# Turn 1 in an order of its own, one sum a slot later, and the transposition ahead of the last sum

## Chip, cores and metric

The kernel runs on one core of one Trainium2 chip. The metric is the device time of one execution in microseconds (us); lower is better.

## The reference

Input x has 8 sequences of 512 tokens with 128 features. Two layers follow one another, each of the form x = x + A(xn) + F(xn), with xn the layer norm of x.

```
layer 0, A: Mamba block.  proj = xn @ in_proj.T (256 + 256 columns); conv over 4 tokens, silu -> u
            x_dbl = u @ x_proj.T -> dt (64), B (16), C (16), each RMS-normed
            dt = softplus(dt @ dt_proj.T + b);  for each of 16 states n:
                h[t] = exp(dt*A_n)[t] * h[t-1] + (dt*u)[t] * B_n[t];   y += h * C_n
            y = (y + u*D) * silu(gate);  out = y @ out_proj.T
layer 0, F: 8 experts (128 -> 512 relu -> 128), each token goes to the one with the largest gate logit
layer 1, A: attention, 16 heads of 8, window of 32 tokens to each side
layer 1, F: silu(x @ wg.T) * (x @ wu.T) @ wd.T, hidden size 384
```

## The kernel before

Every engine has one program, written by one generator of units: `units(it)` yields (name, k, b), unit name with index k for sequence b, and each engine's program emits for each unit what it has to do (or nothing). So one list gives the order of work on TensorE, VectorE, ScalarE, POOL and the DMA queue of SP alike. Engines wait for one another by semaphores.

A lead computes the first layer norm and the expert routing. Then come turns. In turn `it` several sequences are worked on, each at another stage (`LAG`): the lane "pre" prepares sequence it+1 (convolution, u, dt, dtu, B and C rows), "scan" runs the 16 states of sequence it, "attn" runs layer 1 of sequence it-1, and "finish" ends sequence it-2. A turn has 28 slots. `plan()` makes the list of units of each slot from tables, and `PLAN_AT` is that list. `STEP_AT` gives the slot of each of the 16 scan steps, `SUM_AT` the slot of each sum; `EDGE` is the order of slot 0; `HEAD`, `MID` and `REST` place the small units; `SUM_LAST` names the slots in which the sum stands behind row maximum and turn instead of ahead of them.

One state n of the scan goes through these units:

- "step": ScalarE computes the decays dA of state n+1 (line 1105, two instructions), VectorE scans state n (line 884, hst <- dA, dBu).
- "product": VectorE computes dBu of state n+1 (line 876), and POOL computes hc = hst * C (line 1286). It waits until that dBu is done and, since hc has two buffers, until sum n-2 is done.
- "sum": TensorE adds hc into the two banks of y by 8 transposes (line 1389). The last one, of state 15, is "y_end" in slot 0 of the next turn; "gated" (VectorE, line 976) multiplies y by the gate, "yT" (line 1462) transposes it, "init" (line 1380) starts the next y and "out" (line 1471) is the output projection.
- "spread": SP loads the B and C rows of state n+3 into the ring bcr; it waits for product n-1.

Units of "pre": xnT transposes the sequence's input (TensorE, line 1398; ScalarE copies it), hs0 and hs1 are the convolved input projection (TensorE, lines 1406 and 1409), th0 and th1 their tanh (ScalarE, line 1117), u0 and u1 (VectorE, line 904), zg0 and zg1 the gate projection (TensorE, line 1415; its tanh "tg" on ScalarE, line 1122), xdr (VectorE, line 925), dtT, dtp and so on. All of these use one PSUM bank in turn. `take0` lets xnT wait also for the last "fh" (VectorE, line 1041) of the turn before:

```
            if key == "xnT":
                done1(eng, b + LAG["pre"] - 1 - LAG["attn"], f"up{HC - 1}")
```

Units of "attn": x1 adds x_res and the output projection (VectorE, line 980), ln_a the statistics (VectorE, and rstd on POOL, line 1315), ln_b the normalised rows (ScalarE, line 1156; TensorE, line 1478), q and k (TensorE, line 1482; ScalarE), kin the transfer of k into its blocks (SP, line 698), v0 to v3 (TensorE, line 1489). Then 16 blocks, one a slot from slot 5 on: "scores" (TensorE, lines 1502 and 1504, with the values of an earlier block, line 1443), "rowmax" (VectorE, line 1025, nmax), "exp" (ScalarE, line 1185, pexp), "turn" (TensorE, line 1522; ScalarE copies, line 1198). fg, fs, fu and fh are the feed-forward part (lines 1537, 1203, 1036, 1041).

x_res is the input of the sequence plus the experts' rows: "slots" computes the row numbers (VectorE) and loads the input (SP, line 708), "rows" are four indirect transfers of POOL that add the experts' rows to it (line 1267).

Turn 0 has no layer 1 yet; the 40 expert tiles run beside its scan. It also has four slots more, in which scan steps 0 to 4 of sequence 1 are done ahead (`AHEAD`), with sums 0 to 2. So turn 1 skips these and its scan restarts at step 5 in slot 5. For sequence 0, "clear" (VectorE clears kT, line 855, and prepares bias rows), "slots" and "rows" are issued at the end of slot 0 of turn 1, once all expert tiles are stored. The last turn has a list of its own and no scan.

## Time and profile before

| | |
|---|---|
| median of 3 timed runs | 990.7 us (987.13 to 991.66) |
| profiled execution | 994.0 us, of it 992.2 us span from the first to the last instruction |
| TensorE clock granted, mean | 0.926 of full |
| busy: TensorE, VectorE, ScalarE, POOL | 83%, 76%, 64%, 47% |
| turns 2 to 6 | about 95 us each, starting near 350, 446, 544, 638, 733 us |
| turn 1 | from 246 to about 350 us |

The time is that of whole executions; the profile is one further execution, and all positions are counted from its span's start. Busy says how long an engine worked, not that it set the time: which engine waits for which in a stretch says that.

### The profile page before, as it was taken

How to read it: one execution, taken by the hardware profiler on the slowest of the kernel's cores; microseconds unless marked ns; L12 is line 12 of the kernel's file. 1: busy time of each engine (PE TensorE's matmuls, PEld its weight loads, DVE VectorE, ACT ScalarE, POOL GpSimd, SP SyncE). 2: the span in 40 equal slices, each digit the busy share in tenths (PEclk: the TensorE clock that was granted, in tenths of full speed). 3: DMA queues.
4: the chain of work that ended last, by engine and by line, in shares of the span. 5: the costliest groups of instructions: out<-in, count | busy, mean ns of one | idle time of the engine just before them, and what ended most of it. 6: DMA issues, size and time to landing. Idle time of an engine off the chain costs nothing.

```text
span 992.2 us, 15627 instructions
## 1 busy us (share of the span) xinstructions
PE 819.9 (83%) x5226; PEld 566.6 (57%) x5226; DVE 749.5 (76%) x1051; ACT 636.4 (64%) x1976; POOL 462.9 (47%) x256
## 2 busy tenths in 40 slices
PE   4746789767499888989897989898989897888876
PEld 4523787656365456556655665665566555556544
DVE  8719654627258889798879988888889888886577
ACT  1114567535278867875797779667947794885555
POOL 4275242213437447644764575348445843664100
PEclk9967999989699899998899999899989998899898
DMA  8436699785324244424532443444344525551100
GB/s 264 170 102 180 218 281 298 231 239 168 74 68 105 72 109 133 98 72 126 144 92 79 137 132 77 107 118 126 70 110 123 118 59 131 123 132 32 23 1 22
DMA packets 85951, 123.19 MB, mean 124 GB/s; under 512 B 8560, under 2 KB 43760, under 8 KB 85744
## 3 DMA queue, kind: packets, MB, share of 16 engines
q1 hardware_dynamic: 79584, 115.38, 42.2%
q0 software_dynamic: 6288, 6.82, 3.1%
q8 instruction: 42, 0.69, 0.3%
q14 instruction: 37, 0.30, 0.1%
HBM read 106.21 MB, written 12.29 MB: 119 GB/s over the span
## 4 chain that ended last, share of the span: by engine, by line
PE 38%; DVE 23%; issue 15%; POOL 11%; ACT 9%; DMA 3%; DVEq 0%; SPq 0%; POOLq 0%; ACTq 0%
DVE hst L884 8%; POOL hc L1286 6%; PE more L1522 5%; DVE dBu L876 4%; PE y_bank L1389 4%; ACT pexp L1185 3%; POOL xs_d L1252 2%; ACT dA L1105 2%; PE y_bank L1380 2%; PE work L1504 2%; PE work L1409 2%; PE work L1435 1%; POOL x_res L1267 1%; PE work_l L1504 1%; PE work L1415 1%
## 5 line engine op out<-in xcount | busy, mean ns | idle before, releaser
L1286 POOL TENSOR_TENSOR hc<-hst,bcr 128x1024 f32<-128x1024 f32 x124 | 303.3, 2446 | 371.1 <-DVE dBu L876 354.8
L884 DVE TENSOR_TENSOR_SCAN hst<-dA,dBu 128x1024 f32<-128x1024 f32 x128 | 291.7, 2279 | 1.1 <-issue 0.3
L876 DVE TENSOR_TENSOR dBu<-dtu,bcr 128x1024 f32<-128x1024 f32 x128 | 164.8, 1288 | 19.3 <-DMA bcr<-bc_d 9.9
L1105 ACT ACTIVATE dA<-dt,neg_a 128x511 f32<-128x511 f32 x256 | 170.7, 725 | 7.9 <-issue 4.4
L1389 PE MATMUL y_bank<-pk,hc 128*128 128x128 f32 x1024 | 142.9, 284 | 31.4 <-POOL hc L1286 31.4
L1389 PEld LDWEIGHTS y_bank<-pk,hc 128*128 128x128 f32 x1024 | 118.6, 145 | 60.6 <-POOL hc L1286 39.4
L1522 PE MATMUL more<-pk,pexp 128*96 128x128 f32 x480 | 111.4, 297 | 26.1 <-ACT pexp L1185 16.9
L1522 PEld LDWEIGHTS more<-pk,pexp 128*96 128x96 f32 x480 | 56.9, 126 | 79.6 <-issue 35.6
L1198 ACT COPY pT<-more 96x512 f32<-96x512 f32 x120 | 69.8, 582 | 23.0 <-PE more L1522 22.8
L1185 ACT ACTIVATE pexp<-work,nmax 128x96 f32<-128x96 f32 x240 | 77.8, 335 | 10.2 <-DVE nmax L1025 10.2
L1185 ACT ACTIVATE pexp<-work_l,nmax 128x96 f32<-128x96 f32 x240 | 78.5, 346 | 4.3 <-DVE nmax L1025 4.3
L1025 DVE TENSOR_REDUCE nmax<-work 128x4 f32<-128x384 f32 x60 | 33.3, 555 | 50.8 <-PE work L1443 41.6
L1409 PE MATMUL work<-xnT,pk 128*128 128x512 f32 x128 | 63.0, 638 | 0.0
L1267 POOL DMA_INDIRECT x_res<-ys_d,slot_b x32 | 56.1, 1754 | 6.0 <-issue 5.3
L1185 ACT ACTIVATION_READ_ACCUMULATOR pexp<-work_l,nmax 128x1 f32 x240 | 50.8, 211 | 0.0
L1504 PE MATMUL work<-kT,qbd 128*128 128x384 f32 x120 | 49.9, 498 | 0.0
L1504 PE MATMUL work_l<-kT,qbd 128*128 128x384 f32 x120 | 49.2, 492 | 0.0
L1185 ACT ACTIVATION_READ_ACCUMULATOR pexp<-work,nmax 128x1 f32 x240 | 48.2, 201 | 0.0
L1409 PEld LDWEIGHTS work<-xnT,pk 128*128 128x128 f32 x128 | 26.9, 210 | 30.0 <-issue 29.2
L1117 ACT ACTIVATE z<-work 128x512 f32<-128x512 f32 x16 | 9.6, 599 | 48.6 <-PE work L1409 43.8
L1025 DVE TENSOR_REDUCE nmax<-work_l 128x4 f32<-128x384 f32 x60 | 32.9, 548 | 8.4 <-PE work_l L1443 8.2
L1122 ACT ACTIVATE tg<-work 128x512 f32<-128x512 f32 x16 | 9.7, 604 | 31.9 <-PE work L1415 31.9
(367 smaller groups left out, 1562.5 us busy)
## 6 DMA issues: line engine op xcount, KB each, us to landing
bcr<-bc_d SPq DMA_DIRECT2D x128, 512.0 KB
qbd<-in_wx SPq DMA_DIRECT2D x8, 578.0 KB
o_all<-in_wx SPq DMA_DIRECT2D x8, 578.0 KB
pT<-in_wx SPq DMA_DIRECT2D x8, 578.0 KB
kT<-in_wx SPq DMA_DIRECT2D x8, 578.0 KB, 4.9
vw<-in_wx SPq DMA_DIRECT2D x8, 578.0 KB, 5.3
xs_d<-dA POOLq DMA_DIRECT2D x1, 2560.0 KB, 12.2
hst<-in_hidden SPq DMA_DIRECT2D x8, 256.0 KB, 4.0
```

The source lines that it names most:

```text
L876: v.tensor_tensor(dBu[:], dtu[par], bcr[n % RING][:, 0:1, :].to_broadcast([P, NH, L]), ALU.mult).then_inc(s_dBu, 1)
L884: v.tensor_tensor_scan(hst[n % 2][:].rearrange("p h t -> p (h t)"), dA[n % 2][:].rearrange("p h t -> p (h t)"), dBu[:].rearrange("p h t -> ...
L1025: v.tensor_reduce(nmax[:, k, :], w1k(b, f"s{k}")[:, 0:RG * KW].rearrange("p (r k) -> p r k", r=RG), AX_X, ALU.max, negate=True).then_inc(s ...
L1105: s.activation(dA[n % 2][:, h, 1:L], dt[par][:, h, 1:L], ACT.Exp, scale=neg_a[:, h, n:n + 1]).then_inc(s_dA, 1)
L1185: last = s.activation(pexp[k % 2][:, r, :], w1k(b, f"s{k}")[:, r * KW:(r + 1) * KW], ACT.Exp, bias=nmax[:, k, r:r + 1], accum_out=den[:, r ...
L1198: s.copy(pT[k % 4][:], w1k(b, f"pT{k}")[0:KW, :]).then_inc(free1(b, f"pT{k}"), 1)
L1267: g_.indirect_dma_start(x_res[:, j, :], None, ys_d.rearrange("i j p d -> (i j p) d"), bass.IndirectOffsetOnAxis(ap=slot_b[:, j:j + 1], axi ...
L1286: g_.tensor_tensor(hc[n % 2][:], hst[n % 2][:], bcr[n % RING][:, 1:2, :].to_broadcast([P, NH, L]), ALU.mult).then_inc(s_hc, 1)
L1389: last = t.matmul(y_bank[h][:, q], hc[n % 2][:, h, q], ident, is_transpose=True, start=False, stop=(n == N - 1 and j == NT - 1))
L1409: last = t.matmul(bank0[:], w_k[:, k, q], xnT[:, k:k + L], start=False, stop=(k == KC - 1))
L1504: last = t.matmul(w1k(b, key)[:, 0:RG * KW], qbd[:, k, :, :].rearrange("p h q -> p (h q)"), kT[:, :, k * GQ:k * GQ + KW], start=False, sto ...
L1522: last = t.transpose(w1k(b, key)[0:KW, r * P:(r + 1) * P], pexp[k % 2][:, r, :], ident)
```

## The change

It has three parts.

1. Turn 1 gets a plan of its own (`plan_one`, `PLAN_ONE`). Scan steps 5 to 9 stand in slots 0 (5), 1 (6 and 7), 2 (8) and 3 (9), step 5 ahead of the experts' rows of sequence 0; steps 10 to 15 stand in slots 5, 6, 8, 10, 12 and 14. Sums 3 to 7 stand in slots 0 to 3, sums 8 to 13 in the slots of step m+2, sum 14 in slot 16. hs1, th1 and u1 move into slot 1, ahead of x1, q and k. The order of slot 0 is now: sum 3, the edge units, slots, step 5, product 5, spread 5, rows, clear. Clearing now stands behind the rows and behind scan 5.
2. In all turns, sum 7 moves from slot 10 to slot 11, again as the last of the scan and attention units of its slot.
3. In slot 0 of all turns, "xnT" moves ahead of "y_end" and "rdT".

```
--- before.py
+++ after.py
@@ -68,8 +68,8 @@
 SLOTS = 28
 ATTN_AT = 5
 STEP_AT = (0, 1, 2, 3, 4, 5, 6, 8, 10, 12, 14, 16, 18, 20, 22, 23)
-SUM_AT = {m: 1 if m == 0 else STEP_AT[m] + 2 for m in range(N - 1)}
-EDGE = [("attn", "y_end"), ("finish", "rdT"), ("pre", "xnT"), ("attn", "gated"), ("attn", "yT"), ("scan", "init"), ("attn", "out"), ("pre", "hs0")]
+SUM_AT = {m: 1 if m == 0 else STEP_AT[m] + (3 if m == 7 else 2) for m in range(N - 1)}
+EDGE = [("pre", "xnT"), ("attn", "y_end"), ("finish", "rdT"), ("attn", "gated"), ("attn", "yT"), ("scan", "init"), ("attn", "out"), ("pre", "hs0")]
 HEAD = {1: [("attn", "x1", 0), ("attn", "ln_a", 0)], 22: [("attn", "fg", 0), ("attn", "fu", 0)]}
 MID = {2: [("scan", "slots", 0)], 8: [("pre", "ss", 0)], 10: [("pre", "xdr", 0)], 18: [("pre", "dw", 0)], 20: [("pre", "dt", 0)], 23: [("pre", "dtu", 0)]}
 REST = {1: [("pre", "th0", 0), ("pre", "u0", 0), ("attn", "ln_b", 0)],
@@ -88,7 +88,7 @@
         24: [("attn", "fs", 2), ("attn", "fh", 2), ("attn", "rden", 0)], 25: [("pre", "start", 0)]}
 ROWMAX_FIRST = (5, 6)
 ROWMAX_MID = (8, 20)
-SUM_LAST = (7, 8, 10)
+SUM_LAST = (7, 8, 11)
 O_LAG = 3
 HEADS_AT = 1
 O_LAST = 4
@@ -101,7 +101,7 @@
 LAG = {"pre": -1, "scan": 0, "attn": 1, "late": 2, "finish": 2}
 
 
-def plan():
+def plan(step_at, sum_at):
 
     def of(kind, slot):
 
@@ -113,7 +113,7 @@
     slots = []
     for slot in range(SLOTS):
         units = []
-        n = STEP_AT.index(slot) if slot in STEP_AT else None
+        n = step_at.index(slot) if slot in step_at else None
         if slot == 0:
             units += [(lane, name, 0) for lane, name in EDGE]
         units += HEAD.get(slot, [])
@@ -130,7 +130,7 @@
         if n is not None:
             units.append(("scan", "product", n))
         units += [(lane, "averages", g) for lane, g in of("values", slot)]
-        sums = [("scan", "sum", m) for m in range(N - 1) if SUM_AT[m] == slot]
+        sums = [("scan", "sum", m) for m in range(N - 1) if sum_at[m] == slot]
         units += sums if slot not in SUM_LAST else []
         if slot not in ROWMAX_FIRST + ROWMAX_MID:
             units += [(lane, "rowmax", g) for lane, g in of("scores", slot)]
@@ -143,8 +143,32 @@
     return slots
 
 
-PLAN_AT = plan()
+PLAN_AT = plan(STEP_AT, SUM_AT)
 PLAN = [unit for units in PLAN_AT for unit in units]
+
+
+def plan_one():
+
+    steps = {10: 5, 11: 6, 12: 8, 13: 10, 14: 12, 15: 14}
+    step_at = [steps.get(n, SLOTS) for n in range(N)]
+    sum_at = {m: step_at[m + 2] if m + 2 in steps else 16 if m == N - 2 else SLOTS for m in range(N - 1)}
+    slots = plan(step_at, sum_at)
+
+    def scan(n):
+
+        return ("scan", "step", n), ("scan", "product", n), ("scan", "spread", n)
+    step, product, spread = zip(*[scan(n) for n in range(N)])
+    slots[0] = [("scan", "sum", 3)] + slots[0] + [("first", "slots", 0), step[5], product[5], spread[5]] + [
+        ("first", "rows", j) for j in range(NT)] + [("first", "clear", 0)]
+    slots[1] = [("pre", "th0", 0), ("scan", "sum", 4), step[6], ("pre", "u0", 0), ("pre", "hs1", 0), product[6], spread[6],
+                ("pre", "th1", 0), ("scan", "sum", 5), step[7], ("pre", "u1", 0), ("attn", "x1", 0), ("attn", "ln_a", 0),
+                product[7], spread[7], ("attn", "ln_b", 0)]
+    slots[2] = [("attn", "q", 0), ("attn", "k", 0), step[8], ("scan", "slots", 0), product[8], ("scan", "sum", 6), spread[8]]
+    slots[3] = [("attn", "kin", 0), ("attn", "v0", 0), ("attn", "v1", 0), step[9], product[9], ("scan", "sum", 7), spread[9]]
+    return slots
+
+
+PLAN_ONE = plan_one()
 
 
 def last_turn():
@@ -231,7 +255,6 @@
             put(0, slot, ("up", m))
         if 1 <= m <= NM:
             put(0, slot, ("down", m - 1))
-    put(1, 0, ("clear", 0), ("slots", 0), *[("rows", j) for j in range(NT)])
     return at
 
 
@@ -575,7 +598,10 @@
                 for name, k, b in LAST:
                     yield name, k, b, (B - b) % 2
             for slot in range(0 if it >= B else SLOTS_0 if it == 0 else SLOTS):
-                for lane, name, k in PLAN_AT[slot] if slot < SLOTS else []:
+                for lane, name, k in (PLAN_ONE if it == 1 else PLAN_AT)[slot] if slot < SLOTS else []:
+                    if lane == "first":
+                        yield name, k, 0, 0
+                        continue
                     if it == 1 and (name, k) in DONE_AHEAD:
                         continue
                     b = it - LAG[lane]
```

## Rows read from the trace of the kernel before

**Rows 1.** The page's busy table: busy us, share of the span, instructions.

```profile
PE 819.9 (83%) x5226; PEld 566.6 (57%) x5226; DVE 749.5 (76%) x1051; ACT 636.4 (64%) x1976; POOL 462.9 (47%) x256
```

**Rows 2.** Windows: PE, PEld, DVE, ACT, POOL busy us (instructions), clock, DMA.

```profile
249.00:284.00 35.00, 22.73 (x87) 14.54 (x86) 7.42 (x27) 11.81 (x20) 9.59 (x8) 0.71 0.29 69
...
284.00:303.00 19.00, 16.24 (x118) 11.13 (x117) 18.76 (x23) 14.69 (x56) 12.86 (x7) 1.00 0.26 66
303.00:328.00 25.00, 24.84 (x176) 14.09 (x176) 19.66 (x21) 23.09 (x92) 14.86 (x8) 1.00 0.49 109
328.00:346.00 18.00, 14.17 (x84) 7.86 (x83) 16.02 (x14) 15.22 (x43) 7.06 (x3) 0.81 0.21 67
```

**Rows 3.** VectorE's timeline, front of turn 1: start, us, line, operation, [idle before].

```profile
249.03 1.98 DVE L855 MEMSET kT<- 128x2304 f32 x1 [0.43 <-issue]
...
265.42 0.69 DVE L980 TENSOR_TENSOR x1r<-x_res,work 128x512 f32<-128x512 f32 x1 [12.27 <-DMA x_res<-ys_d,slot_b]
...
280.39 0.69 DVE L904 SCALAR_TENSOR_TENSOR u<-z,work 128x512 f32<-128x512 f32 x1 [12.02 <-ACT z L1117]
284.47 2.28 DVE L884 TENSOR_TENSOR_SCAN hst<-dA,dBu 128x1024 f32<-128x1024 f32 x1
286.85 1.23 DVE L876 TENSOR_TENSOR dBu<-dtu,bcr 128x1024 f32<-128x1024 f32 x1
```

**Rows 4.** Timelines of TensorE, SP and POOL, front of turns 1 and 2.

```profile
251.36 3.75 PE L1471 MATMUL work<-pk,dtu 128*128 128x128 f32 x16 [0.77 <-ACT dtu L1152]
...
276.05 3.60 PE L1409 MATMUL work<-xnT,pk 128*128 128x512 f32 x8
...
355.57 1.95 PE L1471 MATMUL work<-pk,dtu 128*128 128x128 f32 x16
...
277.61 2.54 SPq L698 DMA_DIRECT2D kT<-rbuf  x4
...
255.63 0.19 POOL L1266 TENSOR_TENSOR tick_p<-one 128x1 f32<-128x1 f32 x1 [4.78 <-DMA x_res<-in_hidden]
```

**Rows 5.** TensorE's timeline, sum 7 and block 7, turns 3 and 5.

```profile
491.98 1.97 PE L1389 MATMUL y_bank<-pk,hc 128*128 128x128 f32 x8 [2.09 <-POOL hc L1286]
...
498.29 0.33 PE L1502 MATMUL work_l<-bandb,identb 128*128 128x384 bf16 x1
...
683.40 1.09 PE L1389 MATMUL y_bank<-pk,hc 128*128 128x128 f32 x8 [2.25 <-POOL hc L1286]
...
687.52 0.34 PE L1502 MATMUL work_l<-bandb,identb 128*128 128x384 bf16 x1
```

**Rows 6.** VectorE's timeline at the same place in turn 3.

```profile
490.02 0.66 DVE L925 TENSOR_TENSOR xdr<-work,rr 128x256 f32<-128x256 f32 x3
490.60 2.42 DVE L876 TENSOR_TENSOR dBu<-dtu,bcr 128x1024 f32<-128x1024 f32 x1
...
497.91 0.56 DVE L1025 TENSOR_REDUCE nmax<-work 128x4 f32<-128x384 f32 x1 [4.43 <-PE work L1443]
```

**Rows 7.** Timelines at turn 3's edge, and one row of turn 2's.

```profile
445.48 1.10 PE L1389 MATMUL y_bank<-pk,hc 128*128 128x128 f32 x8 [2.33 <-POOL hc L1286]
...
446.97 1.06 PE L1398 MATMUL work<-pk,x_in 128*128 128x128 f32 x4
...
445.49 0.69 DVE L1041 TENSOR_TENSOR fh<-fsg,work 128x512 f32<-128x512 f32 x1
...
447.67 1.27 DVE L976 TENSOR_TENSOR dtu<-y_bank,sg 128x512 f32<-128x512 f32 x2
...
351.14 0.63 PE L1398 MATMUL work<-pk,x_in 128*128 128x128 f32 x4
```

**Rows 8.** Chain of waits, end of turn 1: start, us, what.

```profile
335.74 1.24 ACT dA L1105 x2
...
349.71 0.12 DVE fh L1041
...
351.90 0.69 DVE dtu L976
```

More of the change, by code:

```diff
@@ L70 @@
 STEP_AT = (0, 1, 2, 3, 4, 5, 6, 8, 10, 12, 14, 16, 18, 20, 22, 23)
-SUM_AT = {m: 1 if m == 0 else STEP_AT[m] + 2 for m in range(N - 1)}
-EDGE = [("attn", "y_end"), ("finish", "rdT"), ("pre", "xnT"), ("attn", "gated"), ("attn", "yT"), ("scan", "init"), ("attn", "out"), ("pre", "hs0")]
+SUM_AT = {m: 1 if m == 0 else STEP_AT[m] + (3 if m == 7 else 2) for m in range(N - 1)}
+EDGE = [("pre", "xnT"), ("attn", "y_end"), ("finish", "rdT"), ("attn", "gated"), ("attn", "yT"), ("scan", "init"), ("attn", "out"), ("pre", "hs0")]
 HEAD = {1: [("attn", "x1", 0), ("attn", "ln_a", 0)], 22: [("attn", "fg", 0), ("attn", "fu", 0)]}
@@ L90 @@
 ROWMAX_MID = (8, 20)
-SUM_LAST = (7, 8, 10)
+SUM_LAST = (7, 8, 11)
 O_LAG = 3
@@ L101, with plan @@
 LAG = {"pre": -1, "scan": 0, "attn": 1, "late": 2, "finish": 2}
-def plan():
+def plan(step_at, sum_at):
     def of(kind, slot):
@@ L115, in plan @@
         units = []
-        n = STEP_AT.index(slot) if slot in STEP_AT else None
+        n = step_at.index(slot) if slot in step_at else None
         if slot == 0:
@@ L132, in plan @@
         units += [(lane, "averages", g) for lane, g in of("values", slot)]
-        sums = [("scan", "sum", m) for m in range(N - 1) if SUM_AT[m] == slot]
+        sums = [("scan", "sum", m) for m in range(N - 1) if sum_at[m] == slot]
         units += sums if slot not in SUM_LAST else []
@@ L143, in plan, with plan_one, scan @@
     return slots
-PLAN_AT = plan()
+PLAN_AT = plan(STEP_AT, SUM_AT)
 PLAN = [unit for units in PLAN_AT for unit in units]
+def plan_one():
+    steps = {10: 5, 11: 6, 12: 8, 13: 10, 14: 12, 15: 14}
+    step_at = [steps.get(n, SLOTS) for n in range(N)]
+    sum_at = {m: step_at[m + 2] if m + 2 in steps else 16 if m == N - 2 else SLOTS for m in range(N - 1)}
+    slots = plan(step_at, sum_at)
+    def scan(n):
+        return ("scan", "step", n), ("scan", "product", n), ("scan", "spread", n)
+    step, product, spread = zip(*[scan(n) for n in range(N)])
+    slots[0] = [("scan", "sum", 3)] + slots[0] + [("first", "slots", 0), step[5], product[5], spread[5]] + [
+        ("first", "rows", j) for j in range(NT)] + [("first", "clear", 0)]
+    slots[1] = [("pre", "th0", 0), ("scan", "sum", 4), step[6], ("pre", "u0", 0), ("pre", "hs1", 0), product[6], spread[6],
+                ("pre", "th1", 0), ("scan", "sum", 5), step[7], ("pre", "u1", 0), ("attn", "x1", 0), ("attn", "ln_a", 0),
+                product[7], spread[7], ("attn", "ln_b", 0)]
+    slots[2] = [("attn", "q", 0), ("attn", "k", 0), step[8], ("scan", "slots", 0), product[8], ("scan", "sum", 6), spread[8]]
+    slots[3] = [("attn", "kin", 0), ("attn", "v0", 0), ("attn", "v1", 0), step[9], product[9], ("scan", "sum", 7), spread[9]]
+    return slots
+PLAN_ONE = plan_one()
 def last_turn():
@@ L233, in early @@
             put(0, slot, ("down", m - 1))
-    put(1, 0, ("clear", 0), ("slots", 0), *[("rows", j) for j in range(NT)])
     return at
@@ L577, in units @@
             for slot in range(0 if it >= B else SLOTS_0 if it == 0 else SLOTS):
-                for lane, name, k in PLAN_AT[slot] if slot < SLOTS else []:
+                for lane, name, k in (PLAN_ONE if it == 1 else PLAN_AT)[slot] if slot < SLOTS else []:
+                    if lane == "first":
+                        yield name, k, 0, 0
+                        continue
                     if it == 1 and (name, k) in DONE_AHEAD:
```

## The prediction

> **What bounds the kernel now.** I read the page's busy table first. TensorE is busy 83% and VectorE 76% of the span [rows 1], so neither fills it, and the question is where each waits. I then cut the span at the turns and cut turn 1 finer [rows 2]. It has three parts. From 249 to 284 us VectorE works 7.4 of 35 us and TensorE's mean clock is 0.71: nobody is the bound there, a chain of waits is. From 284 to 303 VectorE works 18.8 of 19. From 303 to 328 TensorE works 24.8 of 25. From 328 to 346 no engine is full, and the chain of waits passes through ScalarE and VectorE.
>
> The first part is a pause of the scan. VectorE waits 12.3 us until the experts' rows are in x_res, does x1 and the statistics, waits 12.0 us for the second tanh (its input projection stands behind q and k on TensorE [rows 4]), and runs scan 5 only at 284.47, behind the row maximum of block 0 [rows 3]. The later turns have no such hole, but have a smaller one of their own. In turn 3 sum 7 keeps TensorE idle 2.09 us, the work behind it runs at half speed (sum 1.97 us, against 1.09 in turn 5), and VectorE waits 4.43 us for block 6 [rows 5, 6]. I find this wait in turns 2 to 6, at half speed after it in all but turn 5. At the turn's edge TensorE waits again, 2.33 us, for the last product of POOL [rows 7].
>
> **Part 1, the own order of turn 1.** Nothing is taken away; five scans (2.28 us) with their five dBu (1.23 us), 17.5 us of VectorE, move from slots 5 to 23 into the 24.3 us in which VectorE idles [rows 3]. Five products of POOL and five pairs of decays (1.24 us each on ScalarE) [rows 8] move too, and SP's five ring loads. What may be late through this is x1. Ahead of it on VectorE now stand, from 248.7 on, scan 5, dBu 6, the clearing (the 1.98 us memset and some 2 us of small copies [rows 3]), scan 6, u0, dBu 7, scan 7 and u1. Their own times are 3 x 2.28 + 2 x 1.23 + 4 + 2 x 0.68 = 14.7 us, so 263.4 without waits. With the waits for the two tanh I get 265.0 to 266, against 265.42 now. On POOL product 5 (2.35 us) comes after dBu 6, at 252.5, and is done at 254.9; the rows start at 255.6 as before [rows 4]. Product 6 follows them at 263.6 to 266, ahead of rstd, which wants the statistics at 267.8. On SP load 8 is queued behind the load of x_res, load 9 waits for product 5. Loads 10 and 11 wait for products 6 and 7 and stand ahead of kin; product 7 is done at about 271.5, and kin waits until 277.6 for k anyway. So rows, x1 and layer norm keep their times within 1 us.
>
> The second projection (3.60 us [rows 4]) then no longer stands between k and v0, which would give 4 us. But the kin transfers are issued from 277.61 for 2.54 us [rows 4] and I take some 2 us more for the last to land, so block 0 can't start before 282.1 against 282.98. ScalarE has two more pairs of decays among the copies, and scan 9 with dBu 10 stands ahead of row maximum 0. I take a gain of 0.3 us for the front; the bounds are a loss of 3.5 (that scan and dBu fully exposed) and a gain of 0.9.
>
> From 284 to 303 the slots hold the same work as before with other step numbers, and VectorE is full: no gain. At slot 10 the sum is now one whose product is two steps old. TensorE's wait of 2.1 us there goes, but VectorE's slow dBu 9 (2.42 us) is next, and row maximum 5 gates exp 5. I work out 1.0 us for slots 10 and 12.
>
> Slots 16 to 23 lose all scans. The chain of waits passes there through two pairs of dA (1.24 us each [rows 8]), a table load, and two scans with a dBu each (2.28 and 1.23 us [rows 3]). I walked the stretch again without them, each engine in order. exp 13 starts 0.95 us earlier, exp 15 2.9, fg1 4.1. The last fh, now at 349.71, would end at 344.95 instead of 350.40. Behind it rden and dBu 0 take 1.7 us, and gated comes at 346.7 against 351.9 [rows 8]: 5.2 us. It is ScalarE, exp by exp and two table loads, that now sets this pace. Bounds: 2 us (if TensorE falls to half speed in the thinner stretch, where it is busy 14.2 of 18 us already [rows 2]) and 7 us. Part 1 is 0.3 + 1.0 + 5.2 = 6.5 us, from 0 to 9.
>
> **Part 2, sum 7 one slot later.** In turn 3 xdr ends near 490.7 [rows 6]. The gate projection can then start, block 6 follows to 492.9, and row maximum 5 ends at 493.5 (dBu 9 ends at 493.0 [rows 6]). exp 5 and turn 5 end at 495.1, sum 7 at 496.0, and block 7 starts there instead of 498.29 [rows 5]: 2.3 us. VectorE's second row maximum comes 4 us earlier, but from here TensorE is the bound as in turn 1, so 2.3 is the gain. Product 9 on POOL needs sum 7 and can't start before dBu 10, near 498, so nothing is late. In turn 5, at full speed, the same walk puts block 7 at 687.4 against 687.52 [rows 5]: 0.1 to 0.2 us. So almost all of this part is the clock, and it is worth something only where the two short waits that stay (0.9 us for xdr, 1.0 us for exp 5) don't bring it down too. Turn 1 and turn 5 show that 2.1 to 2.3 us idle sometimes leaves it up. I take three of four turns kept up: 3 x 2.3 + 2 x 0.2 = 7.3 us, bounds 1 and 9.6. Turns 0 and 7 have no such wait: nothing.
>
> **Part 3, transposition ahead of the last sum.** The time of 4 transposes (0.63 us at full, 1.06 at half speed) goes from behind the sum to before it. But xnT first waits for the last fh (take0), and that ends at 446.18 in turn 3, while the last sum now starts at 445.48 [rows 7]. The sum then starts at 446.8 and ends at 447.8 at best; gated on VectorE now starts at 447.67, freed by dBu. So full speed costs 0.2 us. In turns 3, 5 and 6 the transposes already run at half speed (1.06 us [rows 7]); there the idle stretch grows from 2.33 to 3.0 us, and if sum and transposes both are slow the sum ends near 449 and gated is 1.2 us late. In turn 2 there is nothing to wait for after part 1. I take 3 x 1.2 + 0.2 = 3.8 us of loss, bounds 0 and 6. The earlier copy on ScalarE gives nothing back: hs0, its reader, runs after init and out.
>
> The Trainium skill ("TensorE: Matmul & The Clock Gate", Part 1) says that TensorE is throttled to half by default and that activity releases it. By that rule part 3, which lengthens an idle stretch, costs its upper bound at each edge (rival (c)), and part 2 pays; the trace agrees in that four of five waits at sum 7 are followed by half speed.
>
> **Sum.** 6.5 + 7.3 - 3.8 = 10.0 us less. The profiled execution took 994.0 us around a span of 992.2, so it would be 984.0; the three timed runs have a median of 990.7, 3.3 lower, and I forecast 990.7 - 10.0 = 980.7.
>
> **Rivals.** (a) The clock falls at sum 7's place anyway, since the waits for xdr and exp 5 take its place: part 2 gives 1, and 990.7 - 6.5 - 1 + 3.8 gives 987. For it speaks that 1.9 of 2.1 us idle stay; against it that they are split. (b) Everything goes well: the clock stays up at sum 7 in all four turns and at the edges nothing is lost, 6.5 + 9.6 - 0.2 gives 974.8; with front and end of turn 1 at their best, 972. For it: the edges of turns 2 and 4 ran at full speed. (c) The other side: low clock at the turn's edge. If every one of five edges drops and stays low through the output projection (3.75 us at half speed in turn 1, 1.95 at full in turn 2 [rows 4]), an edge costs 1.3 + 1.8 = 3.1 us, 15.5 in all, against 13.8 gained: 992; with part 2 lost as well, 999. It decides from 2.8 us an edge. Against it: in turn 3 the projection is at full speed again. (d) The front of turn 1 eats its gain: decays 9 and scan 9 put row maximum 0 3.5 us later, and the end of the turn is held by half speed at 2: turn 1 gives nothing and the time is 990.7 - 7.3 + 3.8 = 987.
>
> **How the numbers follow.** Forecast 0.53, (a) 0.17, (b) 0.12, (c) 0.08, (d) 0.10. 0.5% is 5.0 us, about what a measurement of this kernel can tell from no change: faster is below 985.7, slower above 995.7. The forecast's own range is 974 to 986; nearly all of it and (b) are faster, some 0.1 of (a) and (d) too: 0.74. Slower is the worse half of (c) and a little more, 0.06; the rest, 0.20, is the same. The range for 8 in 10 runs from (b) to a little above (a) and (d): 972 to 989.
>
> **What would show it.** In the profile after: scans 5 to 9 of turn 1 before 284 and row maximum 0 at 283 to 285; no scan after slot 14, and the first gated of turn 2 near 346 instead of 351.9; no TensorE wait of 2.1 us on sum 7, and L1415's waits (ACT tg) down; turns 2 to 6 some 1 to 2 us shorter each than 95; before the last sum of each turn a wait of 3 us that now ends with the transposes, freed by fh. Wrong would be: x1 after 267; half speed in the gate projections in spite of the move; the span from the last fh to gated longer by more than 1.5 us.

## The result, and the profile after

The changed kernel took 981.98 us (median of 20 runs, 977.26 to 991.18), the kernel before 989.11 us (20 runs, 983.83 to 994.0). The ratio is 0.9935 with a 95% interval of 0.9912 to 0.9957: 6.4 us by the ratio (4.3 to 8.7), 7.1 by the medians, so it is faster by a small amount that is clear of the noise. The forecast was 980.7, inside a range of 972 to 989. The experiments below show that the total came near for reasons that are not those of the sum: one term was worth nothing, one about 12 us where 7.3 was forecast, and one cost 6 to 10 us where 3.8 was.

The profiled execution took 983.53 us. First the page of the changed kernel: the span, the busy table, and the group of the sums.

```profile
span 981.7 us, 15627 instructions
...
PE 808.1 (82%) x5226; PEld 557.4 (57%) x5226; DVE 757.3 (77%) x1051; ACT 638.4 (65%) x1976; POOL 466.8 (48%) x256
...
L1415 PE MATMUL y_bank<-pk,hc 128*128 128x128 f32 x1024 | 139.4, 279 | 9.8 <-POOL hc L1312 9.5
```

The same group of before has this row on its page (lines of the changed kernel are 26 higher from `plan_one` on).

```profile
L1389 PE MATMUL y_bank<-pk,hc 128*128 128x128 f32 x1024 | 142.9, 284 | 31.4 <-POOL hc L1286 31.4
```

TensorE's idle time ahead of the sums fell from 31.4 to 9.8 us. That is 21.6 us of waits gone for 6.4 us of time: a wait that goes is not time that is won. The count of instructions is as in [rows 1]; TensorE is busy 11.8 us less with the same work, so part of it ran faster, and the mean granted clock is 0.943 against 0.926.

**Front of turn 1.** VectorE's timeline (start, duration, line, operation, idle time before it), to be held against [rows 3].

```profile
248.01 2.35 DVE L1085 TENSOR_TENSOR slot_b<-slot_f,one 128x4 uint32<-128x4 f32 x1
...
254.36 1.98 DVE L881 MEMSET kT<- 128x2304 f32 x1 [0.47 <-issue]
...
268.04 0.69 DVE L930 SCALAR_TENSOR_TENSOR u<-z,work 128x512 f32<-128x512 f32 x1 [3.21 <-ACT z L1143]
268.65 0.68 DVE L1006 TENSOR_TENSOR x1r<-x_res,work 128x512 f32<-128x512 f32 x1
...
282.97 2.29 DVE L910 TENSOR_TENSOR_SCAN hst<-dA,dBu 128x1024 f32<-128x1024 f32 x1 [6.27 <-ACT dA L1131]
...
287.35 0.56 DVE L1051 TENSOR_REDUCE nmax<-work 128x4 f32<-128x384 f32 x1 [0.76 <-PE work L1530]
```

And two rows of TensorE: the bias rows of the second input projection with the wait ahead of them, and the projection, hs1.

```profile
261.43 0.61 PE L1432 MATMUL work<-onesb,conv_rows 96*128 96x512 bf16 x1 [4.82 <-DVE u L930]
261.83 5.47 PE L1435 MATMUL work<-xnT,pk 128*128 128x512 f32 x8
```

Scans 5 to 9 now do stand ahead of the attention blocks; VectorE's hole is filled. But x1 comes at 268.65 against 265.42, and row maximum 0 at 287.35 against 283.99. Counted from the last add of the experts (247.81 here, 248.32 before), x1 is 3.7 us later (20.84 against 17.1) and row maximum 0 is 3.9 us later (39.54 against 35.67). The chain to read is hs1, then the second tanh, then u1, then x1. The projection takes 5.47 us, part of it at half speed, where it took 3.60 [rows 4]; it stands behind 4.82 us in which TensorE waits for u0 (the one PSUM bank of this lane is free only then). u1 waits 3.21 us for its tanh, and x1, whose data could have come sooner, stands directly behind u1 on the same engine.

**Turn 1 after that.** Windows of the changed kernel, columns as in [rows 2].

```profile
248.00:287.00 39.00, 25.45 (x119) 16.36 (x118) 28.02 (x37) 18.73 (x32) 20.77 (x13) 0.82 0.45 111
...
287.00:306.00 19.00, 17.34 (x127) 11.35 (x125) 18.41 (x22) 14.66 (x56) 14.54 (x8) 1.00 0.45 108
...
306.00:331.00 25.00, 22.94 (x160) 12.37 (x152) 15.43 (x19) 20.86 (x87) 13.74 (x7) 1.00 0.35 74
...
331.00:347.00 16.00, 12.62 (x68) 5.33 (x67) 8.00 (x11) 12.54 (x40) 0.00 (x0) 0.89 0.00 1
```

Its last fh and the first gated of turn 2, on VectorE:

```profile
347.27 0.69 DVE L1067 TENSOR_TENSOR fh<-fsg,work 128x512 f32<-128x512 f32 x1
...
349.60 0.69 DVE L1002 TENSOR_TENSOR dtu<-y_bank,sg 128x512 f32<-128x512 f32 x1
```

The last window (16 us against 18 in [rows 2]) has no POOL work and half the VectorE work: all scans are out of it. From row maximum 7 (312.03, before 309.58) to the last fh (347.27, before 349.71 [rows 8]) it is 35.24 us against 40.13, 4.9 us less, where 5.2 was forecast. The middle gained 0.9, where 1.0 was forecast. In all, this one execution has turn 1 1.8 us shorter: 101.79 us from the last add to gated, against 103.58.

**Sum 7.** TensorE's timeline at that place in turn 3, against [rows 5].

```profile
486.81 1.16 PE L1441 MATMUL work<-pk,xnT 128*128 128x128 f32 x8 [0.85 <-DVE xdr L951]
487.80 0.33 PE L1528 MATMUL work<-bandb,identb 128*128 128x384 bf16 x1
...
490.17 1.19 PE L1548 MATMUL more<-pk,pexp 128*96 128x128 f32 x4 [1.04 <-ACT pexp L1211]
491.20 1.04 PE L1415 MATMUL y_bank<-pk,hc 128*128 128x128 f32 x8
492.07 0.33 PE L1528 MATMUL work_l<-bandb,identb 128*128 128x384 bf16 x1
```

The 2.09 us wait is split into 0.85 for xdr and 1.04 for exp 5, as walked, and sum 7 takes 1.04 us instead of 1.97. In turn 5 the clock fell in spite of the move: the gate projection there takes 2.08 us instead of the 1.16 of turn 3.

```profile
675.25 2.08 PE L1441 MATMUL work<-pk,xnT 128*128 128x128 f32 x8 [1.02 <-DVE xdr L951]
```

**The edge.** TensorE's timeline at turn 3's edge and turn 4's, against [rows 7].

```profile
440.62 1.08 PE L1424 MATMUL work<-pk,x_in 128*128 128x128 f32 x4 [3.13 <-issue]
441.50 1.91 PE L1415 MATMUL y_bank<-pk,hc 128*128 128x128 f32 x8
...
537.01 0.63 PE L1424 MATMUL work<-pk,x_in 128*128 128x128 f32 x4 [3.12 <-issue]
537.47 1.04 PE L1415 MATMUL y_bank<-pk,hc 128*128 128x128 f32 x8
```

The idle stretch is 3.13 us instead of 2.33. The profile names no releaser for it, but the transposes start 0.1 us behind the end of the last fh (440.52), for which they wait in the program. At turn 3's edge the transposes run at half speed behind it, and now the last sum does too: 1.91 us against 1.10. From the end of the last fh to gated it is then 2.9 us (440.52 to 443.45), against 1.5 before: late by 1.4. The low clock behind gated is not new at this edge, though. These are the windows of the 7 us from gated on in the changed kernel and in the kernel before:

```profile
443.45:450.45 7.00, 6.34 (x33) 6.20 (x33) 4.71 (x4) 3.88 (x7) 2.10 (x1) 0.54 0.38 101
```

```profile
447.67:454.67 7.00, 6.54 (x36) 6.20 (x35) 4.71 (x5) 4.21 (x7) 2.11 (x1) 0.58 0.60 152
```

At turn 4's edge both run at full speed behind an idle stretch of the same length.

The time from each gated to the next puts this together. "Half" is what the mean clock of that stretch says of time at half speed: 2 x (1 - clock) x length.

| turn | 2 | 3 | 4 | 5 | 6 | sum |
|---|---|---|---|---|---|---|
| before, us | 95.77 | 97.20 | 94.02 | 95.09 | 96.27 | 478.35 |
| before, half | 7.8 | 12.7 | 4.5 | 6.3 | 10.9 | 42.2 |
| after, us | 93.85 | 95.10 | 92.72 | 96.26 | 94.69 | 472.62 |
| after, half | 3.8 | 6.5 | 0.5 | 10.9 | 5.9 | 27.6 |

A turn that ran wholly at full speed takes some 92.5 us, and every turn above that has stretches at half speed. Turn 5, the one that kept its clock at sum 7 before, lost it there after, and became slower by 1.2 us. So a single profile cannot price these edits. That is why each part was timed by itself.

### The profile page after: what moved, and what is told of

Same layout as the page of the kernel before. It is cut to its first block, busy times and chain, and to the rows that moved or that the text cites. A ratio compares the mean times of both kernels' runs of the same rounds, so it can differ in the third digit from the quotient of the medians.

```text
span 981.7 us, 15627 instructions
## 1 busy us (share of the span) xinstructions
PE 808.1 (82%) x5226; PEld 557.4 (57%) x5226; DVE 757.3 (77%) x1051; ACT 638.4 (65%) x1976; POOL 466.8 (48%) x256
## 4 chain that ended last, share of the span: by engine, by line
PE 49%; DVE 20%; issue 10%; ACT 9%; DMA 4%; POOL 4%; SPq 3%; DVEq 0%; POOLq 0%; ACTq 0%
DVE hst L910 8%; PE y_bank L1415 6%; PE more L1548 6%; PE work L1435 4%; DVE dBu L902 3%; ACT pexp L1211 3%; POOL xs_d L1278 2%; PE y_bank L1406 2%; PE work L1530 2%; PE work_l L1530 2%; DMA bcr<-bc_d 2%; DVE nmax L1051 2%; PE work L1461 2%; ACT dA L1131 1%; PE work L1497 1%
## 5 line engine op out<-in xcount | busy, mean ns | idle before, releaser
L902 DVE TENSOR_TENSOR dBu<-dtu,bcr 128x1024 f32<-128x1024 f32 x128 | 168.2, 1314 | 18.5 <-DMA bcr<-bc_d 9.6
L1415 PE MATMUL y_bank<-pk,hc 128*128 128x128 f32 x1024 | 139.4, 279 | 9.8 <-POOL hc L1312 9.5
L1435 PE MATMUL work<-xnT,pk 128*128 128x512 f32 x128 | 65.7, 661 | 0.0
L1293 POOL DMA_INDIRECT x_res<-ys_d,slot_b x32 | 60.2, 1882 | 5.7 <-issue 5.6
L1441 PE MATMUL work<-pk,xnT 128*128 128x128 f32 x128 | 20.6, 311 | 11.8 <-DVE xdr L951 10.4
```

The costliest lines, as they stand in the source:

```text
L902: v.tensor_tensor(dBu[:], dtu[par], bcr[n % RING][:, 0:1, :].to_broadcast([P, NH, L]), ALU.mult).then_inc(s_dBu, 1)
L1293: g_.indirect_dma_start(x_res[:, j, :], None, ys_d.rearrange("i j p d -> (i j p) d"), bass.IndirectOffsetOnAxis(ap=slot_b[:, j:j + 1], axi ...
L1415: last = t.matmul(y_bank[h][:, q], hc[n % 2][:, h, q], ident, is_transpose=True, start=False, stop=(n == N - 1 and j == NT - 1))
L1435: last = t.matmul(bank0[:], w_k[:, k, q], xnT[:, k:k + L], start=False, stop=(k == KC - 1))
```

## The experiments

All kernels compute the whole reference. "Zeros" in some of them are matmuls that add zero to y. The time is the median of the runs, the ratio is to the kernel before with its 95% interval, the clock is the median over the runs of the mean granted clock.

### Each part alone

The first three kernels tell which terms of the sum hold. Part 2 alone (e1):

```
+SUM_AT = {m: 1 if m == 0 else STEP_AT[m] + (3 if m == 7 else 2) for m in range(N - 1)}
+SUM_LAST = (7, 8, 11)
```

> The kernel before with part 2 alone: sum 7 in slot 11 instead of 10, in all turns. Theory (the wait at sum 7 costs through TensorE's clock): the wait of 2.1 us before sum 7 is gone in turns 2 to 6, the gate projection of these turns runs at full speed in at least three of four turns that had half speed, and the time falls by 5 to 9 us (ratio 0.991 to 0.995). Rival (the wait is only handed on to xdr and exp 5, and the gain of the changed kernel is from turn 1 and the later clock): the time falls by 0 to 2 us, and the gate projections stay at half speed. In both, turn 1 keeps its pause.

Part 3 alone (e2):

```
+EDGE = [("pre", "xnT"), ("attn", "y_end"), ("finish", "rdT"), ("attn", "gated"), ...
```

> The kernel before with part 3 alone: xnT ahead of the last sum and rdT. Theory (xnT waits for the last fh, and so holds up the last sum): TensorE idles about 3 us instead of 2.3 at the edges of turns 3 to 6, gated is released by the sum instead of standing behind dBu, 0.2 us later at full and 1.3 us later at half speed; the time grows by 1 to 4 us (ratio 1.001 to 1.004). Rival (the place of the four transposes makes no difference, since gated stands behind dBu anyway): within 1 us. A third way, that the earlier copy on ScalarE helps, would make it shorter by 1 to 2 us.

Part 1 alone (e3) is `plan_one` with SUM_AT, SUM_LAST and EDGE as before.

> The kernel before with part 1 alone: the own order of turn 1. From the trace of the changed kernel, x1 comes 3.2 us late and row maximum 0 3.4 us late, slots 10 and 12 give 0.9 and the end of the turn 4.9, so the first gated of turn 2 comes 2.3 us sooner: 2 to 3 us less in all (ratio 0.997 to 0.998). Rival (the front's loss belongs to the edge's new order or to a chance state of the clock in that one profile): row maximum 0 near 284 and 5 to 7 us less in all.

| | us (runs) | ratio | clock |
|---|---|---|---|
| before | 988.21 (22) | | 0.9335 |
| e1, part 2 alone | 977.58 (6) | 0.9877 [0.984, 0.9913] | 0.943 |
| e2, part 3 alone | 998.95 (6) | 1.0104 [1.0064, 1.0144] | 0.9195 |
| e3, part 1 alone | 989.05 (12) | 1.0014 [0.9984, 1.0044] | 0.935 |

Part 2 gives 12 us (8.6 to 15.8 by its interval) where 7.3 was forecast; the upper bound of 9.6 lies inside the interval. Part 3 costs 10 us (6.3 to 14.2) where 3.8 was forecast, above its bound of 6. Part 1 gives nothing that can be told from zero where 6.5 was forecast. The expectations of the first two were missed on the high side too (5 to 9 and 1 to 4 us), and e3's 2 to 3 us did not come. Without part 3 the change would be a better one; that is tried below.

Where part 2's surplus lies can be read by cutting each turn in three at rows of VectorE: from gated to row maximum 5, from there to row maximum 8 (sum 7 and what stands behind it), and from there to the next gated. In turn 3 of the kernel before, whose gated is at 447.67, and then of part 2 alone:

```profile
492.93 0.54 DVE L1025 TENSOR_REDUCE nmax<-work_l 128x4 f32<-128x384 f32 x1
...
503.21 0.56 DVE L1025 TENSOR_REDUCE nmax<-work 128x4 f32<-128x384 f32 x1
```

```profile
444.76 1.28 DVE L976 TENSOR_TENSOR dtu<-y_bank,sg 128x512 f32<-128x512 f32 x2
...
487.79 0.54 DVE L1025 TENSOR_REDUCE nmax<-work_l 128x4 f32<-128x384 f32 x1
...
495.76 0.56 DVE L1025 TENSOR_REDUCE nmax<-work 128x4 f32<-128x384 f32 x1 [1.44 <-PE work L1443]
```

The same readings, in us, for turns 2 to 6 one by one; the last two columns are summed over them:

| | gated to row maximum 5 | to row maximum 8 | to the next gated | sum |
|---|---|---|---|---|
| before | 44.71, 45.26, 43.02, 45.47, 45.46 | 9.64, 10.28, 9.58, 8.09, 9.38 | 207.46 | 478.35 |
| e1, part 2 alone | 44.72, 43.03, 43.03, 43.34, 44.71 | 7.97, 7.97, 7.97, 7.97, 7.98 | 207.07 | 465.76 |
| e2, part 3 alone | 44.72, 46.40, 45.07, 45.30, 43.03 | 9.58, 9.64, 8.10, 10.29, 9.48 | 209.91 | 481.52 |
| after | 43.03, 45.57, 43.04, 44.98, 45.31 | 7.97, 7.97, 7.97, 9.14, 7.97 | 209.67 | 472.62 |

At sum 7 the kernel before loses 2.3 us in turn 3, which is what the prediction worked out for this place, 1.4 to 1.7 in turns 2, 4 and 6 and 0.1 in turn 5: part 2 gains 7.1 us there. The windows of the 8 us that hold sum 7 in turn 3 show the clock, before and then with part 2 alone:

```profile
490.00:498.00 8.00, 6.02 (x29) 4.50 (x30) 3.57 (x7) 3.42 (x13) 7.72 (x4) 0.57 0.28 76
```

```profile
487.00:495.00 8.00, 6.95 (x56) 4.67 (x54) 7.22 (x7) 6.20 (x24) 7.84 (x5) 1.00 0.45 120
```

A clock of 0.57 over 8 us is 6.9 us at half speed, and TensorE gets through 29 matmuls there against 56. In time these 6.9 us cost only 2.3.

The surplus is elsewhere: 5.1 us come from the first stretch, in turns 3, 5 and 6. The kernel before runs there at half speed from some 1 us ahead of gated to some 6 us behind it, and part 2 alone does not, although its wait for the last product is as long (2.34 us at the edges of turns 3 and 5). The windows of the 7 us from gated on in turn 5, before and then with part 2 alone (turn 3's clock is 0.58 against 0.93):

```profile
638.89:645.89 7.00, 6.54 (x36) 6.21 (x35) 4.70 (x5) 4.21 (x7) 2.12 (x1) 0.59 0.41 131
```

```profile
629.55:636.55 7.00, 6.17 (x45) 5.26 (x46) 6.00 (x10) 4.12 (x7) 2.11 (x1) 1.00 0.47 138
```

So a wait taken away at one place changed the clock at the next edges. Why the clock stays up there is not shown. Over turns 2 to 6 part 2 alone has 15.7 us at half speed against 42.2: 12.6 us less time, about half of the 26.5 us by which the stretch at half speed shrank.

Part 3 alone shows the other side. Its TensorE timeline at turn 3's edge:

```profile
443.37 0.77 PE L1398 MATMUL work<-pk,x_in 128*128 128x128 f32 x4 [3.12 <-issue]
443.93 1.91 PE L1389 MATMUL y_bank<-pk,hc 128*128 128x128 f32 x8
```

In this profile turns 2 to 6 are 3.2 us longer than in the kernel before, 2.5 of it in the last stretch, where gated comes late. That is less than the 10 us: e2's profiled run is its fastest (994.48), and the profiled run of the kernel before is slow for it (994.0 against medians of 987 to 991). So the traces give the places, and the medians the price.

### Is it the clock, or the order?

Two explanations of part 2's gain are left. Either a sum that stands a slot later lets the queue behind it run ahead, or only the missing idle stretch counts, through the clock. e5 is the kernel before, with sum 7 where it was, and matmuls in its wait that add zeros. If the order counts it can only lose, by the work added; if the clock counts it gains like e1.

```
+            def add_zeros(times):
...
+                for k in range(times):
+                    t.matmul(y_bank[k % NH][:], ident, xnT[:, 0:1].to_broadcast([P, L]), start=False, stop=False)
...
+                if n == 7 and 2 <= b <= B - 2:
+                    add_zeros(2)
```

> The kernel before with one addition: in turns 2 to 6 TensorE adds zeros to y with two matmuls of 512 columns, about 0.9 us each, ahead of its wait for the product of sum 7; the result is unchanged and sum 7 stays where it was. Theory (what the wait costs is the clock): sum 7 starts when it did, since the idle time was 2.1 us, but it and the gate projection behind it run at full speed in turns 2 to 6, and the time falls by 5 to 9 us although TensorE does 9 us more work. Rival (sum 7's place in the order is what counts): no gain, within 2 us of the kernel before.

It took 978.81 us (6 runs; the kernel before, run beside it, 986.91, 11 runs), ratio 0.9905 [0.9876, 0.9933], clock 0.9445. Its TensorE timeline in turn 3, with the zeros first:

```profile
485.35 1.89 PE L1386 MATMUL y_bank<-xnT,pk 128*128 128x512 f32 x4
...
487.61 1.09 PE L1396 MATMUL y_bank<-pk,hc 128*128 128x128 f32 x8 [0.37 <-POOL hc L1286]
...
489.43 0.33 PE L1509 MATMUL work<-bandb,identb 128*128 128x384 bf16 x1
```

The sum stands where it stood (42.06 us behind gated, against 44.31 in the kernel before, whose first stretch is 2.25 us longer), and POOL's product ends its wait as before. 1.89 us of that wait are filled with useless work, and the sum runs at full speed (1.09 us against 1.97 [rows 5]) with the gate projection and block 6 right behind. Adding work made the kernel faster by about as much as part 2 did (the intervals overlap). Turns 2 to 6 take 466.18 us in its profile against 465.76 in e1's, and the gain has the same two places, 6.5 us at sum 7 and 5.4 in the first stretch. So part 2's gain is the clock, shown; the order itself gives at most the 0.1 us a turn by which e5 stays above e1 at sum 7.

The same question for part 3's loss: e11 is part 3 alone, with zeros while xnT waits.

```
                 if name == "xnT":
+                    if 3 <= b < B:
+                        add_zeros(3 if b > 3 else 2)
```

> The kernel before with part 3 and matmuls of zeros while xnT waits, three at the edges of turns 3 to 6 and two at that of turn 2. Part 3 alone took 10.3 us more. Theory (clock): most of this is given back, the time is within 3 us of the kernel before. Rival (the order itself costs): it stays 7 us or more above.

It took 988.74 us (12 runs), ratio 0.997 [0.994, 1.0], clock 0.933; without the zeros it was 1.0104 and 0.9195. TensorE's timeline at turn 3's edge, first the zeros with the work they follow:

```profile
441.26 2.75 PE L1386 MATMUL y_bank<-xnT,pk 128*128 128x512 f32 x6
...
444.55 0.63 PE L1405 MATMUL work<-pk,x_in 128*128 128x128 f32 x4 [0.55 <-issue]
445.02 1.04 PE L1394 MATMUL y_bank<-pk,hc 128*128 128x128 f32 x8
```

The windows over the same 9 us of that edge, part 3 alone and then with the zeros:

```profile
443.00:452.00 9.00, 7.97 (x44) 7.58 (x45) 6.57 (x7) 4.47 (x8) 1.23 (x1) 0.62 0.56 151
```

```profile
443.00:452.00 9.00, 7.69 (x58) 6.42 (x57) 7.88 (x9) 5.46 (x10) 1.70 (x2) 1.00 0.59 186
```

TensorE is busy about the same 8 us, but at a clock of 0.62 it gets through 44 matmuls and at 1.00 through 58 (the two kernels are not at the same point to the microsecond; the clock is the reading). The time is back at that of the kernel before with the order of part 3. This alone does not show that all of the loss was the clock, because the zeros also lift half speed that the kernel before has at these edges: its clock over the matching 9 us of turn 3 is 0.62 as well.

```profile
444.79:453.79 9.00, 7.63 (x39) 7.06 (x40) 7.48 (x8) 5.39 (x10) 1.86 (x2) 0.62 0.66 188
```

The pair e8 and e10 below has the zeros at the edges with and without part 3, and settles it.

### The front of turn 1

The profile after says that x1 is late because it stands behind u1. Rival (d) says that scan 9 and dBu 10 ahead of row maximum 0 make it late. e4 is the changed kernel with x1 and ln_a ahead of scan 7 and u1; the scans keep their slots.

```
-                ("pre", "th1", 0), ("scan", "sum", 5), step[7], ("pre", "u1", 0), ("attn", "x1", 0), ("attn", "ln_a", 0),
+                ("pre", "th1", 0), ("scan", "sum", 5), ("attn", "x1", 0), ("attn", "ln_a", 0), step[7], ("pre", "u1", 0),
```

> The changed kernel with one edit in slot 1 of turn 1: x1 and ln_a stand ahead of scan 7 and u1. Theory A (the front is late because x1 stands behind u1, whose input projection waits for u0 and then runs at half speed): x1 starts as soon as the rows are in, near 266, row maximum 0 near 284, and the time is 3 to 4 us below that of the changed kernel, some 9 to 11 us below the kernel before. Theory B (scan 9 and dBu 10, which stand ahead of row maximum 0 and wait for the decays behind the copy of k, hold it up): x1 is early, row maximum 0 stays near 287, and the time is that of the changed kernel.

It took 980.48 us (11 runs), ratio 0.9905 [0.9874, 0.9936], clock 0.943. VectorE's timeline:

```profile
263.45 0.69 DVE L1006 TENSOR_TENSOR x1r<-x_res,work 128x512 f32<-128x512 f32 x1 [3.20 <-DMA x_res<-ys_d,slot_b]
...
276.72 2.29 DVE L910 TENSOR_TENSOR_SCAN hst<-dA,dBu 128x1024 f32<-128x1024 f32 x1 [3.41 <-ACT dA L1131]
...
281.59 0.56 DVE L1051 TENSOR_REDUCE nmax<-work 128x4 f32<-128x384 f32 x1 [1.24 <-PE work L1530]
```

x1 waits for its transfer again, as it did before the change, and row maximum 0 comes 36.03 us behind the last add (245.56) against 39.54: 3.5 us sooner, although a scan still waits 3.41 us for its decays in front of it. The cause is x1's place, not scan 9; already in the changed kernel row maximum 0 waits 0.76 us for TensorE behind that scan and dBu 10. In time e4 gives 3 us by the ratios (0.9905 against 0.9935), with intervals that overlap.

### Without part 3, and the best of all

e7 is the changed kernel with EDGE as before and x1 first; e8 is e7 with two zero matmuls ahead of the last sum of sequences 2 to 6, which stands at the edges of turns 3 to 7, to ask whether the half speed that the edges keep in e7 costs anything.

> The changed kernel without part 3 (xnT behind rdT as before) and with x1 and ln_a ahead of scan 7 and u1 in turn 1. Part 2 alone took 10.6 us off; the own order of turn 1 with x1 first ends turn 1 3.8 us sooner. If the parts add up, the time is 13 to 15 us below the kernel before (974 to 976). If the new edge is harmless beside part 2, as the small loss in the changed kernel would have it, it is that of the changed kernel with x1 first, 979 to 981.

```
+                if n == N - 1 and 2 <= b <= B - 2:
+                    add_zeros(2)
```

> The kernel of the run before this one (no part 3, x1 first) with two matmuls that add zeros to y (1.8 us) ahead of the last sum of turns 2 to 6, within its wait of 2.3 us. Theory (clock): the sum and what follows the edge run at full speed in every turn, the periods of turns 2 to 6 come near 92.4 us each, and the time is 1 to 4 us below that of the run before. Rival (the edges of that kernel keep their clock anyway): the same time, or up to 1 us longer where the zeros reach into the sum.

e7 took 970.97 us (5 runs), ratio 0.9834 [0.9817, 0.9852], clock 0.950. It beats both kernels: about 16 us under the one before, 10 under the changed one. e8 took 971.42 us (6 runs), 0.9836 [0.9809, 0.9864], clock 0.954: no gain. Two turns of e7's profile that began with half speed at the edge took 92.48 and 92.52 us, within 0.1 us of its shortest. In both the half speed ends within 1.3 us behind gated. In turn 3 of e1 it does too: the last sum takes 1.97 us there, and the turn 92.40. So half speed ahead of gated costs nothing in the old order, in which gated stands behind dBu anyway. Where it lasts to some 6 us behind gated, as in turns 3, 5 and 6 of the kernel before, it costs 2.2 to 2.5 us.

### Part 3's price beside the others

e6 is the changed kernel with three zero matmuls ahead of xnT's wait at the edges of turns 3 to 6. e10 is the same with x1 first, so e7 plus part 3 plus zeros.

```
                 if name == "xnT":
+                    if 4 <= b < B:
+                        add_zeros(3)
```

> The changed kernel with one addition: at the edges of turns 3 to 6 TensorE adds zeros to y with three matmuls of 512 columns (2.6 us) while xnT waits 3.1 us for the last fh. Theory (part 3 costs mainly by the clock that falls behind the longer idle stretch): no low clock in the 12 us behind gated, each edge that had it gains 2.5 us, and the time falls by 4 to 8 us below the changed kernel. Rival (part 3 costs because the sum is late, whatever the clock): within 1.5 us of the changed kernel.

> The changed kernel with x1 first and with the three matmuls of zeros while xnT waits at the edges of turns 3 to 6. It differs from the kernel without part 3 and with x1 first (971.0 us, ratio 0.9834) only by part 3 and its zeros. Theory (the loss of part 3 is the clock): 970 to 974 us, ratio 0.983 to 0.987. Rival (part 3 costs by itself, whatever the clock): 976 to 980 us, ratio 0.989 to 0.992.

e6 took 979.11 us (6 runs), 0.9927 [0.9905, 0.995], clock 0.948: inconclusive, since the 4 to 8 us that were expected did not come in the median, although turns 2 to 5 of its profile took 92.6 us each. e10 took 973.28 us (6 runs), 0.9836 [0.9797, 0.9874], clock 0.952. It differs from e8 (0.9836) by part 3 and by the place and number of the zeros. With the waits at the edges filled in both, part 3 costs nothing that can be told; their profiles have 464.31 and 463.80 us for turns 2 to 6, so the order itself costs 0.1 to 0.2 us an edge. That is what shows part 3's loss to be the clock. e6 and e10 differ by x1's place alone, and their intervals allow 3 us between them, which is what e4 gave for it. So e6's median may only be high by chance; that stays open.

The last two leave one part out each: e9 is the changed kernel without part 3, e12 the changed kernel with turn 1 as before.

> The changed kernel without part 3: xnT behind rdT as before, with parts 1 and 2. Theory (part 3 is what the changed kernel loses most by): 3 to 8 us below the changed kernel (ratio to the kernel before 0.986 to 0.990), with more of the execution at full clock. Rival (part 3 costs only in the kernel before, where low clock follows sum 7 too): within 2 us of the changed kernel (0.992 to 0.995).

> Parts 2 and 3 on the kernel before, turn 1 as it was. If the effects add up (10.6 less for part 2, 10.3 more for part 3) the time is that of the kernel before, ratio 0.998 to 1.002, and part 1 is worth 5 to 6 us beside them. If part 3 costs less beside part 2, the ratio is 0.992 to 0.997 and part 1 is worth 0 to 3 us.

| | us (runs) | ratio | clock |
|---|---|---|---|
| e9, parts 1 and 2 | 978.06 (6) | 0.9878 [0.9843, 0.9913] | 0.9445 |
| e12, parts 2 and 3 | 982.28 (9) | 0.9937 [0.9904, 0.997] | 0.940 |
| after, all three | 981.98 (20) | 0.9935 [0.9912, 0.9957] | 0.943 |

e9 is e1 (0.9877), and e12 is the changed kernel: part 1 is worth nothing in either pair. x1 first is worth 4.4 us by the ratios here (e9 to e7) and 3 in e4; the intervals overlap in both pairs. Part 3 costs 5.6 us beside part 2 (e9 to after, 0.0057 of 989; e1 to e12 gives 5.9).

Where part 3's loss lies is plainest in e12. Its profiled run is its slowest (990.36), so the sizes are at the high end. At the edges of turns 3 to 6 transposes and sum run at half speed, and VectorE waits for the sum, as here at turn 4's edge, first TensorE, then VectorE:

```profile
540.29 1.08 PE L1398 MATMUL work<-pk,x_in 128*128 128x128 f32 x4 [3.13 <-issue]
541.17 1.91 PE L1389 MATMUL y_bank<-pk,hc 128*128 128x128 f32 x8
```

```profile
543.12 1.29 DVE L976 TENSOR_TENSOR dtu<-y_bank,sg 128x512 f32<-128x512 f32 x2 [1.34 <-PE y_bank L1389]
```

Against e1, gated comes late by 5.9 us in all at these four edges, and 5.8 us more are lost between gated and row maximum 5, where the clock is low again some 14 us behind gated (0.57 from 461 to 465 in turn 3). At sum 7 nothing is lost.

## Why the prediction was right, and where its sum was not

**The total.** 10.0 us less were forecast, 6.4 to 7.1 came. The direction is right. The terms are not, and that they nearly cancel is luck.

**Part 1: forecast 6.5 (0 to 9), measured 1.4 lost** (e3's interval runs from 1.6 us gained to 4.4 lost; e9 and e12 give zero beside the other parts). Two of its three terms are in the profile as walked (0.9 for 1.0, 4.9 for 5.2), but the 0.9 is not part 1's alone: with part 2 alone this stretch of turn 1 shortens as much (25.59 to 24.69 us from row maximum 0 to 7), so beside part 2 it counts only once. The term that failed is the front. The step was "rows, x1 and layer norm keep their times within 1 us", with x1 at 265.0 to 266. My sum had VectorE's own times and some 2 us for both tanh, but not what stands between them: hs1 can't start before u0, which now stands behind two scans, so TensorE idles 4.82 us and then takes 5.47 us for hs1 instead of 3.60. x1 after 267 was named as what would be wrong, and it was 268.65. The loss of 3.9 us is 0.4 over the bound that I had put on it, and e4 shows its cause. Rival (d) had the place right, its mechanism (scan 9 and dBu 10) not. That leaves 1.8 to 2.1 us gained in the profiles of turn 1 (103.58 to 101.79, e3 101.46) that the times don't show. Part of an answer is in the profiles: e9's turn 1 is longer than before (104.86), with a clock of 0.51 from 334 to 344, in the thinner stretch where the prediction had named half speed as the lower bound; and e3's turns 2 to 6 are 2.0 us longer than those of the kernel before. Whether that is typical of their runs is open.

**Part 2: forecast 7.3 (1 to 9.6), measured 12 alone.** The mechanism stands: e5 gives the gain without the move. At sum 7 itself even the size stands, 7.1 us in e1's profile against 7.3, though by two errors that cancel: all four turns kept up instead of three, but three of them had only 1.4 to 1.7 us to give and not 2.3. What the sum put at nothing is the clock at the turn's edge, which part 2 does not touch. It stayed up there in turns 3, 5 and 6 and gave 5.1 us more. In the changed kernel most of that is lost again: turns 3, 5 and 6 take 44.98 to 45.57 us to row maximum 5, about as before. And turn 5 lost its clock at sum 7 behind a wait of 1.02 us, as rival (a) said all turns would. The Trainium skill ("TensorE: Matmul & The Clock Gate", Part 1) has the rule in general, half speed by default and full speed by activity; e5 and e11 agree, with 0.9905 for two matmuls of zeros a turn and 1.0104 to 0.997 for two or three an edge.

**Part 3: forecast a loss of 3.8 (0 to 6), measured 10 alone and 6 beside part 2.** The step that named the danger was right: the idle stretch did grow to 3.1 us, and gated is 1.4 us late in turn 3 where 1.2 was forecast; at full speed the order costs 0.1 to 0.2 us an edge (e8 and e10), where 0.2 was forecast. The term 3 x 1.2 had two things wrong. It took three edges, and e12 has four with 1.34 to 1.35 us. And it stopped at gated, while e12 loses as much again between gated and row maximum 5. That is rival (c) in part; it took the low clock to last through the output projection, 3.1 us an edge with 2.8 as its point of decision. Five edges for 10 us make 2 us each alone, and with 6 us beside part 2 it stayed under that point. Which stretches make up the 10 us of part 3 alone is not shown, because e2's one profile has only 3.2 of them.

**Rivals.** (a) holds in one turn of five. (b) is about what e7 reaches when x1 stands first and part 3 is left out: 971, where (b) said 972 to 975. (c) and (d) both occurred in part and were paid for by part 2's surplus, which came from a place that no rival named. The range added the bounds of three terms as if they were independent; two of them share one cause, the clock of all turns, and a change at one place moved it at others.

**All kernels together.** The product of median time and median clock is 922.5 for the kernel before, 926 for the changed one, 918.5 for e2 (the slowest) and 922.4 for e7 (the fastest). The times differ by 28 us (2.9%), the products of all fourteen kernels lie between 918.5 and 928.2 (1.0%). This is an association. e5, and e8 with e10, are what shows the direction.

## What to carry to other kernels

Where TensorE waits in a full stretch (2 us here), look at the duration of the matmuls behind the wait. Price the wait by the rows behind it, as the prediction did, and then expect the clock to change at later places too: cut every turn at the same rows before and after, and see where the time went. Matmuls of zeros into a bank that is being summed, placed ahead of the wait, are a cheap test of it. Before moving work of one lane to the front of another's chain, list what each shared engine has queued ahead of the chain's next link, here x1 behind u1, and put that link first. Parts of a change that meet in one resource want a run each: all three together hid a loss of 6 us and a term worth nothing. Half speed has no one price: 6.9 us of it cost 2.3 at sum 7, and the part ahead of gated cost nothing in the old order and 1.4 us in the new one.
